# Adapter loops of five engines written out, batch numbers read ahead of SyncE's waits, one role read a pair on TensorE

## The chip, the cores and the metric

The kernel runs on one core of one Trainium2 chip. The metric is the time on the device in microseconds (us). The kernel before took 2073.11 us, the median of three runs (2072.64 to 2078.01).

## The reference, cut to what matters

`reference` chains two layers over `x` of shape (64, 64, 512): 64 batches of 64 tokens of 512 features. The first layer is attention with a projection, a gelu layer of 2048 hidden units (`cW1`, `cW2`), a second gelu layer over the concatenation (`mW1`, `mW2`), and a clip to [0, 1]. The second layer is an adapter whose weights are chosen per batch by a role (one of R = 3 matrices):

```python
h  = einsum('bsh,bhk->bsk', z, W_down[role]) + b_down[role]   # 512 -> 256
u  = einsum('bsk,bkh->bsh', gelu(h), W_up[role]) + b_up[role] # 256 -> 512
y  = z + u
yn = (y - mean(y)) * rsqrt(var(y) + 1e-5)
return yn * gamma[role] + beta[role]
```

Everything is float32. The kernel splits each operand into a high and a low part and forms a product from three matrix products (`mm3`).

## The kernel before, in words

The first layer takes the first 1905 us or so of the program and the diff does not touch it: eight tiles of 512 tokens, worked two at a time in four stages, its instructions written out with no loop. Its result `z` goes to DRAM in batch order (`z_by_batch`), the last two tiles by SyncE's two `store_z` (L444) while the adapter has begun.

The adapter works on pairs of batches with one role: `NPAIR` = 34 pairs of 2 x 64 = 128 token rows. The batches were sorted by role earlier on the chip, so each pair's two batch numbers (`first_t`, `second_t`) and its role (`role_t`) are small integer tables in SBUF. An engine that needs one reads it into a register with `value_load`, which the trace shows as TENSOR_LOAD, FUSED_REGOPS and SEQ_ASSERT on the engine's own sequence. Pair n goes through five engines:

- SyncE (SP), `unit(m)`: waits until slot (m + 2) % 4 of `zs` has been read (`zl_s`, `zf_s`), then `load_z(m + 6)` (L450 reads a batch number and L451 issues the load, twice), then `store_second(m - 1)` (L456 reads a batch number, a wait follows until the first half of that pair has landed, and L459 issues the store of the second half).
- ScalarE (ACT), `unit(n)`: the high part of `ht` (L999), for pair n + 2 the high part `z_hi` (L962) and four instructions `zf` = z + bias (L965) after a role read (L963), and for pair n + 1 the gelu `hs` (L995).
- VectorE (DVE), `unit(n)`: statistics of pair n - 1 (L1599), the low part `ht_lo` (L1630), moments (L1602, L1604), `centre` into `yg` (L1611), `z_lo` of pair n + 2 (L1547), `scale_shift` into `yo` (L1620). `yo` has four slots, and L1620 waits until the second store of pair n - 4 (of its own count) has landed.
- TensorE (PE), `unit(n)`: `turn(n)` reads the role (L1980), waits for `hs`, transposes it (L2001, 2 products) and puts `zf` into the accumulator (L2011, 4 products); `down(n + 1)` reads the role of the next pair, then has one bias product (L1990) and 12 products of `mm3` (L1675 to L1677 into a bank named y); `up(n)` has 6 products of `mm3` (into a bank named x).
- GpSimd (POOL): `inverse_std(n)` (L591) and `store_first(n)` (L595 reads a batch number, L598 issues the store of the first half).

The order on each engine is written by hand, and the engines meet only in counting semaphores. `UNROLL` is 4. Each engine handles its first few pairs in written-out Python, most pairs in one hardware loop (`Fori`) whose body holds four pairs, and the last few written out again: on TensorE the loop takes pairs 4 to 31 in 7 passes, on VectorE 5 to 28, on ScalarE 2 to 29, on GpSimd 0 to 31, on SyncE the units m = 1 to 24 in two loops of 4 and 2 passes. In a loop, table indices and the counts waited for come from registers. All buffers and slots repeat with a period of 1, 2 or 4 pairs.

Of the kernel before, what the change touches and what calls it, by code (L numbers as in the profile page):

```python
# [13 lines left out]
B, S, D = 64, 64, 512  # L14
# [82 lines left out]
NPAIR = B // 2 + 2 * (R // 2)  # L97
NSLOT = 2 * NPAIR
UNROLL = 4
LOOPS = (NPAIR - 3) // UNROLL  # L100


CB1, MB1, BP, CB2, MB2 = 0, JH, 2 * JH, 2 * JH + DC, 2 * JH + 2 * DC
# [3 lines left out]
def program(nc, xT, xk, w1c, w1m, w2c, w2m, wqT, wkT, wvT, wp, bias, target, role,  # L107
# [7 lines left out]
    with ctx:  # L115
# [246 lines left out]
        def _(sp):  # L362
# [80 lines left out]
            def store_z(t, tile, stored):  # L443
                sp.dma_start(z_dram[t * BT:(t + 1) * BT].rearrange("b p f -> p b f"),  # L444
                            tile[:].rearrange("p c n -> p (c n)").rearrange("p (b f) -> p b f", b=BT)
                            ).then_inc(stored, 16)

            def load_z(n, slot):
                for k, table in enumerate((first_t, second_t)):
                    b = sp.value_load(table[0:1, bass.ds(n, 1)], min_val=0, max_val=B - 1)  # L450
                    sp.dma_start(zs[:, slot, k, :, :].rearrange("p c s -> p (c s)"),  # L451
                                 z_dram[bass.ds(b, 1)].rearrange("o p f -> (o p) f")).then_inc(zl[slot], 16)

            def store_second(n, u):

                b = sp.value_load(second_t[0:1, bass.ds(n, 1)], min_val=0, max_val=B - 1)  # L456
                dst = out[bass.ds(b, 1)].rearrange("o s d -> (o s) d")
                sp.wait_ge(a_stored[u % UNROLL], (n - u % UNROLL) * (16 // UNROLL) + 16)
                sp.dma_start(dst, yo[S:2 * S, u % UNROLL, :]).then_inc(b_stored[u % UNROLL], 16)  # L459
# [16 lines left out]
            sp.dma_start(bet[:], beta.to_broadcast([P, R, D])).then_inc(gb_loaded, 16)  # L476

            for n in range(2):
                sp.wait_ge(zl_s, n + 1)
                sp.wait_ge(zf_s, n + 1)  # L480
                load_z(n + 4, n)

            def unit(m, u, load):

                if load:
                    sp.wait_ge(zl_s, m + 3)
                    sp.wait_ge(zf_s, m + 3)
                    load_z(m + 6, (u + 2) % 4)
                if not isinstance(m, int) or m:
                    store_second(m - 1, u + UNROLL - 1)  # L490

            unit(0, 0, True)
# [1 line left out]
            store_z(NT - 2, h2_tile, last_stored[0])  # L494
            sp.wait_ge(z2_ready, DC * NS)
            store_z(NT - 1, h1_tile, last_stored[1])
            sp_loops, sp_early = (NPAIR - 7) // UNROLL, 4
            with sp.Fori(0, sp_early) as k:
                for u in range(UNROLL):
                    unit(k * UNROLL + (u + 1), u + 1, True)  # L500
            sp.wait_ge(last_stored[0], 16)
            sp.wait_ge(last_stored[1], 16)
            with sp.Fori(sp_early, sp_loops) as k:
                for u in range(UNROLL):
                    unit(k * UNROLL + (u + 1), u + 1, True)
            for m in range(sp_loops * UNROLL + 1, NPAIR):
                unit(m, m, m + 6 < NPAIR)
            store_second(NPAIR - 1, NPAIR - 1)
            for u in range(UNROLL):
# [4 lines left out]
        def _(pool):  # L514
# [74 lines left out]
            def inverse_std(n, slot):  # L589
                pool.wait_ge(ve_s, n + 1)  # L590
                nc.gpsimd.tensor_tensor(rstd[:, slot:slot + 1], veps[:, slot:slot + 1], mhalf[:],  # L591
                                        ALU.pow).then_inc(rstd_s, 1)

            def store_first(n, u):
                b = pool.value_load(first_t[0:1, bass.ds(n, 1)], min_val=0, max_val=B - 1)  # L595
                dst = out[bass.ds(b, 1)].rearrange("o s d -> (o s) d")
                pool.wait_ge(yo_s, n + 1)
                pool.dma_start(dst, yo[0:S, u % UNROLL, :]).then_inc(a_stored[u % UNROLL], 16)  # L598

            inverse_std(0, 0)  # L600
            pool_loops = (NPAIR - 2) // UNROLL
            with pool.Fori(0, pool_loops) as k:
                for u in range(UNROLL):
                    store_first(k * UNROLL + u, u)
                    inverse_std(k * UNROLL + (u + 1), (u + 1) % 2)
            for n in range(pool_loops * UNROLL, NPAIR):
                store_first(n, n)
                if n + 1 < NPAIR:
                    inverse_std(n + 1, (n + 1) % 2)
# [40 lines left out]
        def _(act):  # L650
# [302 lines left out]

            def split_z(n, u):

                if isinstance(n, int) and n < 2:
                    act.wait_ge(bu_loaded, 16 * R)
                    act.wait_ge(sorted_s, 3)
                slot = u % 4
                act.wait_ge(zl[slot], (n - slot) * 8 + 32)  # L960
                src = zs[:, slot].rearrange("p k c s -> p c k s")
                nc.scalar.copy(z_hi[:, u % 2].rearrange("p c (k s) -> p c k s", k=2), src).then_inc(zh_s, 1)  # L962
                r = act.value_load(role_t[0:1, bass.ds(n, 1)], min_val=0, max_val=R - 1)  # L963
                for c in range(DC):
                    ins = nc.scalar.activation(zf[:, slot, c, :].rearrange("p (k s) -> p k s", k=2), src[:, c],  # L965
                                               ACT.Identity, bias=bucol[:, bass.ds(r, 1), c])
                ins.then_inc(zf_s, 1)
# [37 lines left out]
            gelu_pair(0, 0)  # L1005
            for n in range(2):
                unit(n, n, True, True)
            with act.Fori(0, LOOPS) as k:
                for u in range(UNROLL):
                    unit(k * UNROLL + (2 + u), 2 + u, True, True)  # L1010
            for n in range(LOOPS * UNROLL + 2, NPAIR):
                unit(n, n, n + 2 < NPAIR, n + 1 < NPAIR)


# [1 line left out]
        def _(dve):  # L1016
# [635 lines left out]
                z2_clip(s, c)  # L1652
            for n in range(3, 5):
                unit(n, n, True, True, False)
            dve_loops = (NPAIR - 7) // UNROLL
            with dve.Fori(0, dve_loops) as k:
                for u in range(UNROLL):
                    unit(k * UNROLL + (5 + u), 5 + u, True, True, True)
            for n in range(dve_loops * UNROLL + 5, NPAIR):
                unit(n, n, n + 2 < NPAIR, True, True)  # L1660
            last = NPAIR - 1
            r = dve.value_load(role_t[0:1, last:last + 1], min_val=0, max_val=R - 1)
# [8 lines left out]
        def _(pe):  # L1671
# [307 lines left out]
            def pair_role(n):  # L1979
                return pe.value_load(role_t[0:1, bass.ds(n, 1)], min_val=0, max_val=R - 1)  # L1980
# [1 line left out]
            def rows(ap, r):  # L1982
                return ap[:, bass.ds(r, 1)].rearrange("p o n -> p (o n)")

            def down(n, u):

                r = pair_role(n)
                pe.wait_ge(zl_s, n + 1)
                ps = d_ps[u % 2][:, 0:KD]
                nc.tensor.matmul(ps, ones2[:], rows(brow[:], r), start=True, stop=False)  # L1990
                for k in range(DC):
                    w = [rows(half[:, :, k, :], r) for half in (wd_hi, wd_lo)]
                    ins = mm3(ps, (z_hi[:, u % 2, k, :], z_lo[:, u % 2, k, :]), w, False, k == DC - 1)
                ins.then_inc(d_mm, 1)

            def turn(n, u):

                r = pair_role(n)
                pe.wait_ge(hgelu_s, n + 1)
                for k in range(KD // P):  # L2000
                    ins = nc.tensor.transpose(ht_ps[u % 2][:, k * P:(k + 1) * P], hs[:, u % 2, k * P:(k + 1) * P],  # L2001
                                              ident[:])
                ins.then_inc(ht_mm, 1)
                ps = u_ps[u % 4]
                if isinstance(n, int) and n < 4:
                    pe.wait_ge(z1_s, (NS - 1) * DC + n + 1)
                else:
                    pe.wait_ge(yg_s, n - 3)
                pe.wait_ge(zf_s, n + 1)
                for k in range(DC):  # L2010
                    nc.tensor.matmul(ps[:, k * P:(k + 1) * P], zf[:, u % 4, k, :], ident[:], start=k == 0,  # L2011
                                     stop=False, is_transpose=True)
                return r

            def up(n, u, r):

                if isinstance(n, int) and n == 0:
                    pe.wait_ge(l1_lo, 2 * R)
                pe.wait_ge(ht_lo_s, n + 1)
                for k in range(KD // P):  # L2020
                    w = [rows(half[:, :, k, :], r) for half in (wu_hi, wu_lo)]
                    cols = slice(k * P, (k + 1) * P)
                    ins = mm3(u_ps[u % 4][:], (ht_hi[:, u % 2, cols], ht_lo[:, u % 2, cols]), w, False,
                              k == KD // P - 1)
                ins.then_inc(u_mm, 1)

            def unit(n, u, d):

                r = turn(n, u)
                if d:  # L2030
                    down(n + 1, u + 1)
                up(n, u, r)

            down(0, 0)
            for n in range(4):
                unit(n, n, True)
            pe_loops = (NPAIR - 5) // UNROLL
            with pe.Fori(0, pe_loops) as k:
                for u in range(UNROLL):
                    unit(k * UNROLL + (4 + u), u, True)  # L2040
            for n in range(pe_loops * UNROLL + 4, NPAIR):
                unit(n, n, n + 1 < NPAIR)


# [46 lines left out]
```

## Time and profile before

| What | Value |
|---|---|
| median of 3 runs | 2073.11 us |
| the profiled execution's own time | 2075.36 us |
| its span | 2073.8 us |
| TensorE busy over the span | 2020.6 us (97%) |
| VectorE, ScalarE, GpSimd busy | 67%, 46%, 5% |
| granted TensorE clock, mean | 0.996 |

The page gives one row for each group of instructions with its busy time, count and mean, and says what ended the idle time ahead of them. The trace can also be asked for a stretch of time, for the chain of waits that ended last in it, and for one engine's instructions in order. The adapter is only the last 160 us or so; the share of busy time over the whole span says almost nothing about it.

### The profile page before, as it was taken

How to read it: one execution, taken by the hardware profiler on the slowest of the kernel's cores; microseconds unless marked ns; L12 is line 12 of the kernel's file. 1: busy time of each engine (PE TensorE's matmuls, PEld its weight loads, DVE VectorE, ACT ScalarE, POOL GpSimd, SP SyncE). 2: the span in 40 equal slices, each digit the busy share in tenths (PEclk: the TensorE clock that was granted, in tenths of full speed). 3: DMA queues.
4: the chain of work that ended last, by engine and by line, in shares of the span. 5: the costliest groups of instructions: out<-in, count | busy, mean ns of one | idle time of the engine just before them, and what ended most of it. 6: DMA issues, size and time to landing. Idle time of an engine off the chain costs nothing.

```text
span 2073.8 us, 28655 instructions
## 1 busy us (share of the span) xinstructions
PE 2020.6 (97%) x9396; PEld 1677.2 (81%) x9397; DVE 1398.5 (67%) x2597; ACT 955.2 (46%) x1977; POOL 99.1 (5%) x184
## 2 busy tenths in 40 slices
PE   7999999999999999999999999999999999999997
PEld 6878888888878888888878888888878888887876
DVE  5676786555777686555777686555677685555886
ACT  4654444433654454333654444333654444334554
POOL 0000000000000000000000000000000000000222
PEclk9999999999999999999999999999999999999999
DMA  4011233215111143215111143215111132114544
GB/s 163 28 52 53 65 129 107 90 49 202 63 51 61 58 136 107 84 54 203 62 51 61 51 142 107 76 62 203 62 52 61 51 122 61 49 44 144 176 123 106
DMA packets 111934, 187.86 MB, mean 91 GB/s; under 512 B 12285, under 2 KB 72192, under 8 KB 107456
## 3 DMA queue, kind: packets, MB, share of 16 engines
q1 hardware_dynamic: 98672, 126.19, 19.4%
q0 software_dynamic: 13136, 60.04, 8.4%
q8 instruction: 72, 1.18, 0.2%
q14 instruction: 54, 0.44, 0.1%
HBM read 145.82 MB, written 40.37 MB: 90 GB/s over the span
## 4 chain that ended last, share of the span: by engine, by line
PE 85%; DVE 7%; SPq 3%; issue 2%; ACT 2%; DMA 1%; ACTq 0%; POOL 0%; DVEq 0%; POOLq 0%
PE y L1675 15%; PE y L1677 15%; PE y L1676 15%; PE x L1675 13%; PE x L1677 12%; PE x L1676 12%; SPq L450 1%; DVE w_lo L1103 1%; PE y L1756 1%; DVE f L1227 1%; PE x L1781 1%; SPq L451 1%; DVE a_forms L1272 1%; DMA w_blocks<-w1c 1%; SPq L459 1%
## 5 line engine op out<-in xcount | busy, mean ns | idle before, releaser
L672 ACT CAST w_hi<-w_blocks 128x512 fp32r<-128x512 f32 (+1 forms) x464 | 231.6, 518 | 131.1 <-PE y L1677 83.6
L1103 DVE TENSOR_TENSOR w_lo<-w_blocks,w_hi 128x512 fp32r<-128x512 f32 (+1 forms) x464 | 249.6, 564 | 56.2 <-ACT w_hi L672 56.2
L1675 PE MATMUL x<-h_hi,w_hi 128*128 128x512 f32 x512 | 199.6, 390 | 3.1 <-ACT f L725 3.1
L1675 PE MATMUL y<-h_hi,w_hi 128*128 128x512 f32 x512 | 199.7, 390 | 1.9 <-ACT p_copy L725 1.9
L1677 PE MATMUL x<-h_hi,w_lo 128*128 128x512 f32 x512 | 199.3, 389 | 0.0
L1677 PE MATMUL y<-h_hi,w_lo 128*128 128x512 f32 x512 | 199.2, 389 | 0.0
L1676 PE MATMUL x<-h_lo,w_hi 128*128 128x512 f32 x512 | 199.2, 389 | 0.0
L1676 PE MATMUL y<-h_lo,w_hi 128*128 128x512 f32 x512 | 199.2, 389 | 0.0
L1675 PE MATMUL y<-a_forms,w_hi 128*128 128x512 f32 x480 | 188.1, 392 | 2.1 <-DVE f L1206 1.2
L1677 PE MATMUL y<-a_forms,w_lo 128*128 128x512 f32 x480 | 186.8, 389 | 0.0
L1676 PE MATMUL y<-a_forms,w_hi 128*128 128x512 f32 x480 | 186.8, 389 | 0.0
L1675 PE MATMUL y<-c_forms,w_hi 128*128 128x512 f32 x448 | 174.3, 389 | 0.0
L1677 PE MATMUL y<-c_forms,w_lo 128*128 128x512 f32 x448 | 174.3, 389 | 0.0
L1676 PE MATMUL y<-c_forms,w_hi 128*128 128x512 f32 x448 | 174.3, 389 | 0.0
L710 ACT CAST w_hi<-w_st 128x512 fp32r<-128x512 f32 x128 | 79.1, 621 | 203.4 <-PE y L1677 109.4
L1675 PE MATMUL x<-a_forms,w_hi 128*128 128x512 f32 x424 | 165.4, 390 | 5.2 <-issue 5.2
L1187 DVE TENSOR_TENSOR h_lo<-f,h_hi 128x512 fp32r<-128x512 f32 x236 | 158.0, 686 | 10.8 <-ACT f L725 10.8
L1677 PE MATMUL x<-a_forms,w_lo 128*128 128x512 f32 x424 | 165.1, 389 | 0.0
L1676 PE MATMUL x<-a_forms,w_hi 128*128 128x512 f32 x424 | 165.0, 389 | 0.0
L1216 DVE TENSOR_TENSOR f<-p_copy,y 128x512 f32<-128x512 f32 x32 | 22.0, 687 | 186.9 <-PE y L1677 186.9
L724 ACT ACTIVATE h_hi<-y,bias_sb 128x512 fp32r<-128x512 f32 x40 | 27.6, 690 | 208.5 <-PE y L1677 208.4
L724 ACT ACTIVATE h_hi<-f,bias_sb 128x512 fp32r<-128x512 f32 x120 | 87.0, 725 | 70.0 <-issue 60.7
(231 smaller groups left out, 4259.9 us busy)
## 6 DMA issues: line engine op xcount, KB each, us to landing
w_blocks<-w1m SPq DMA_DIRECT2D x128, 256.0 KB, 4.2
w_blocks<-w1c SPq DMA_DIRECT2D x64, 256.0 KB, 3.2
w_st<-w2c SPq DMA_DIRECT2D x64, 256.0 KB, 3.3
w_st<-w2m SPq DMA_DIRECT2D x64, 256.0 KB, 4.7
x_hi_lo<-x_halves POOLq DMA_DIRECT2D x6, 2048.0 KB, 11.2
zs<-z_by_batch SPq DMA_DIRECT2D x68, 128.0 KB, 2.1
cms<-f SPq DMA_DIRECT2D x32, 256.0 KB, 2.7
z_cms<-cms POOLq DMA_DIRECT2D x8, 1024.0 KB, 6.4
```

The lines of the kernel that those rows point to most:

```text
L450: b = sp.value_load(table[0:1, bass.ds(n, 1)], min_val=0, max_val=B - 1)
L451: sp.dma_start(zs[:, slot, k, :, :].rearrange("p c s -> p (c s)"), z_dram[bass.ds(b, 1)].rearrange("o p f -> (o p) f")).then_inc(zl[slot], 16)
L459: sp.dma_start(dst, yo[S:2 * S, u % UNROLL, :]).then_inc(b_stored[u % UNROLL], 16)
L672: nc.scalar.copy(w1_hi[:, w % RING, cols], src).then_inc(w1_hi_s, 1)
L710: nc.scalar.copy(w2_hi[:, j, :], w2_st[:, j, :]).then_inc(w2_hi_s, 1)
L724: nc.scalar.activation(hidden_dst(which)[0], src, ACT.Gelu, bias=bias)
L1103: nc.vector.tensor_tensor(w1_lo[:, w % RING, cols], src, f32(w1_hi[:, w % RING, cols]), ALU.subtract).then_inc(w1_lo_s, 1)
L1187: nc.vector.tensor_tensor(lo, half_f32(gi), f32(hi), ALU.subtract).then_inc(hlo_s, 1)
L1216: nc.vector.tensor_tensor(f1[:, 1, :], pc[:, Q % 2, :], GB[Q // NQ % 2][2][:], ALU.add).then_inc(sum_s, 1)
L1675: nc.tensor.matmul(ps, w[0], x[0], start=first, stop=False, skip_group_check=more)
L1676: nc.tensor.matmul(ps, w[0], x[1], start=False, stop=False, skip_group_check=more)
L1677: return nc.tensor.matmul(ps, w[1], x[0], start=False, stop=last, skip_group_check=more)
```

## The change

Every `Fori` of the adapter is gone: the five engines' instruction sequences for all 34 pairs are written out by Python, so the indices and counts are constants. The work of each pair and the slots are the same. Two orders change. On SyncE `load_z` now reads both batch numbers first, then waits for the slot, then issues both loads (the waits have moved from `unit` into `load_z`). On TensorE the role of pair n + 1 is read once, ahead of `turn(n)`, and kept for `up(n + 1)`; before, it was read in `down(n + 1)` and again in `turn(n + 1)`.

```diff
+            def batch_of(table, n):
+                return sp.value_load(table[0:1, n:n + 1], min_val=0, max_val=B - 1)
+
             def load_z(n, slot):
-                for k, table in enumerate((first_t, second_t)):
-                    b = sp.value_load(table[0:1, bass.ds(n, 1)], min_val=0, max_val=B - 1)
+                batches_ = [batch_of(table, n) for table in (first_t, second_t)]
+                if n >= 4:
+                    sp.wait_ge(zl_s, n - 3)
+                    sp.wait_ge(zf_s, n - 3)
+                for k, b in enumerate(batches_):
                     sp.dma_start(zs[:, slot, k, :, :].rearrange("p c s -> p (c s)"),
                                  z_dram[bass.ds(b, 1)].rearrange("o p f -> (o p) f")).then_inc(zl[slot], 16)
 ...
             def unit(m, u, load):
 
                 if load:
-                    sp.wait_ge(zl_s, m + 3)
-                    sp.wait_ge(zf_s, m + 3)
                     load_z(m + 6, (u + 2) % 4)
 ...
-            sp_loops, sp_early = (NPAIR - 7) // UNROLL, 4
-            with sp.Fori(0, sp_early) as k:
-                for u in range(UNROLL):
-                    unit(k * UNROLL + (u + 1), u + 1, True)
-            sp.wait_ge(last_stored[0], 16)
-            sp.wait_ge(last_stored[1], 16)
-            with sp.Fori(sp_early, sp_loops) as k:
-                for u in range(UNROLL):
-                    unit(k * UNROLL + (u + 1), u + 1, True)
-            for m in range(sp_loops * UNROLL + 1, NPAIR):
+            for m in range(1, NPAIR):
+                if m == 4 * UNROLL + 1:
+                    sp.wait_ge(last_stored[0], 16)
+                    sp.wait_ge(last_stored[1], 16)
                 unit(m, m, m + 6 < NPAIR)
 ...
-            with pool.Fori(0, pool_loops) as k:
-                for u in range(UNROLL):
-                    store_first(k * UNROLL + u, u)
-                    inverse_std(k * UNROLL + (u + 1), (u + 1) % 2)
-            for n in range(pool_loops * UNROLL, NPAIR):
+            for n in range(NPAIR):
 ...
-            with act.Fori(0, LOOPS) as k:
-                for u in range(UNROLL):
-                    unit(k * UNROLL + (2 + u), 2 + u, True, True)
-            for n in range(LOOPS * UNROLL + 2, NPAIR):
+            for n in range(2, NPAIR):
 ...
-            with dve.Fori(0, dve_loops) as k:
-                for u in range(UNROLL):
-                    unit(k * UNROLL + (5 + u), 5 + u, True, True, True)
-            for n in range(dve_loops * UNROLL + 5, NPAIR):
+            for n in range(5, NPAIR):
 ...
-            def down(n, u):
-
-                r = pair_role(n)
+            def down(n, u, r):
+
                 pe.wait_ge(zl_s, n + 1)
 ...
             def turn(n, u):
 
-                r = pair_role(n)
                 pe.wait_ge(hgelu_s, n + 1)
 ...
-            down(0, 0)
-            for n in range(4):
-                unit(n, n, True)
-            pe_loops = (NPAIR - 5) // UNROLL
-            with pe.Fori(0, pe_loops) as k:
-                for u in range(UNROLL):
-                    unit(k * UNROLL + (4 + u), u, True)
-            for n in range(pe_loops * UNROLL + 4, NPAIR):
-                unit(n, n, n + 1 < NPAIR)
+            r = pair_role(0)
+            down(0, 0, r)
+            for n in range(NPAIR):
+                if n + 1 < NPAIR:
+                    r_next = pair_role(n + 1)
+                turn(n, n)
+                if n + 1 < NPAIR:
+                    down(n + 1, n + 1, r_next)
+                up(n, n, r)
+                r = r_next
```

## Rows read from the trace of the kernel before

**Rows 1.** VectorE in order of time (start us, us), statistics of pairs 4 and 11

```profile
1945.02 0.70 DVE L1599 BATCH_NORM_STATS2 st<-x 128x6 f32<-128x512 f32 x1 [1.32 <-PE x L1677]
...
1970.71 0.70 DVE L1599 BATCH_NORM_STATS2 st<-x 128x6 f32<-128x512 f32 x1 [0.17 <-PE x L1677]
```

**Rows 2.** The same, statistics of pair 32

```profile
2057.85 0.70 DVE L1599 BATCH_NORM_STATS2 st<-x 128x6 f32<-128x512 f32 x1 [0.64 <-PE x L1677]
```

**Rows 3.** Chain that ended last, 1958 to 2036 us, shares by line

```profile
by line: SPq L450 25.5%; issue 22.5%; SPq L451 17.1%; SPq L459 11.8%; SPq L456 10.0%; DMA zs<-z_by_batch 2.5%; PE x L2011 1.1%; PE y L1675 1.0%; PE y L1990 1.0%; ACTq L963 0.8%; PE y L2001 0.8%; ACT zf L965 0.8%; PE y L1677 0.8%; PE y L1676
```

**Rows 4.** SyncE in order of time, whole span of the loops and after

```profile
1973.50 1.52 SPq L451 DMA_DIRECT2D zs<-z_by_batch  x2
...
1990.47 1.52 SPq L451 DMA_DIRECT2D zs<-z_by_batch  x2
...
2044.38 1.46 SPq L451 DMA_DIRECT2D zs<-z_by_batch  x2
...
2047.95 1.65 SPq L451 DMA_DIRECT2D zs<-z_by_batch  x2
```

**Rows 5.** Line L450, loop units 5 to 24 (duration ns min/median/max)

```profile
L450 SPq TENSOR_LOAD <-first_t x20: 263/494/739, 1955.7 to 2035.6; - x20
```

**Rows 6.** Line L450, written-out units 25 to 27

```profile
L450 SPq TENSOR_LOAD <-first_t x3: 263/269/282, 2039.7 to 2047.2; - x3
L450 SPq TENSOR_LOAD <-second_t x3: 267/272/470, 2040.8 to 2048.3; - x3
```

**Rows 7.** DMA queues, 1980.80 to 1981.30 us, during a slow batch read

```profile
q0 software_dynamic: 29, 0.12, 113.7%
```

**Rows 8.** TensorE in order of time, bias products around a loop's return

```profile
1952.63 0.36 PE L1990 MATMUL y<-brow,ones 128*128 x1
...
1956.63 0.38 PE L1990 MATMUL y<-brow,ones 128*128 x1
```

**Rows 9.** The same, pairs 5 to 7, and the wait ahead of pair 5

```profile
1941.77 0.38 PE L1990 MATMUL y<-brow,ones 128*128 x1 [0.82 <-issue]
...
1945.39 0.36 PE L1990 MATMUL y<-brow,ones 128*128 x1
1949.00 0.38 PE L1990 MATMUL y<-brow,ones 128*128 x1
```

**Rows 10.** Chain in order of time, TensorE, two pairs (start us, us, what)

```profile
2039.34 0.28 issue
2039.63 0.38 PE y L1990
...
2042.60 0.24 PE x L1677
...
2043.49 0.12 PE y L1990
```

**Rows 11.** VectorE in order of time, first and last of pair 6's seven instructions

```profile
1952.26 0.70 DVE L1599 BATCH_NORM_STATS2 st<-x 128x6 f32<-128x512 f32 x1
...
1954.93 0.75 DVE L1620 SCALAR_TENSOR_TENSOR yo<-yg,rstd,bet 128x512 f32<-128x512 f32 x1
```

**Rows 12.** Who waited for whom, 1970 to 2026 us (us in total, times, longest)

```profile
ACT z_hi L962 <- DMA zs<-z_by_batch: 9.8, 13, 1.3
...
DVE yo L1620 <- DMA out<-yo: 4.3, 13, 0.6
```

**Rows 13.** The same, 1944 to 1970 us

```profile
ACT z_hi L962 <- DMA zs<-z_by_batch: 0.4, 1, 0.4
```

**Rows 14.** DMA issues, 1956 to 2044 us, with median us to landing

```profile
zs<-z_by_batch SPq DMA_DIRECT2D x42, 128.0 KB, 2.0
```

**Rows 15.** DMA queues of the whole span, from the page (packets, MB, share)

```profile
q8 instruction: 72, 1.18, 0.2%
```

**Rows 16.** Busy time by stretch: us, PE, PEld, DVE, ACT, POOL (instructions), clock, DMA

```profile
1750.00:1800.00 50.00, 50.00 (x222) 41.41 (x221) 28.96 (x45) 17.33 (x29) 0.00 (x0) 1.00 0.21 64
1970.00:2026.00 56.00, 52.14 (x329) 43.02 (x329) 45.20 (x92) 33.42 (x93) 14.68 (x26) 1.00 0.45 123
```

More of the change, by code:

```diff
@@ L99 @@
 UNROLL = 4
-LOOPS = (NPAIR - 3) // UNROLL
 CB1, MB1, BP, CB2, MB2 = 0, JH, 2 * JH, 2 * JH + DC, 2 * JH + 2 * DC
@@ L454, in store_second @@
             def store_second(n, u):
-                b = sp.value_load(second_t[0:1, bass.ds(n, 1)], min_val=0, max_val=B - 1)
+                b = batch_of(second_t, n)
                 dst = out[bass.ds(b, 1)].rearrange("o s d -> (o s) d")
@@ L478, in _ @@
             for n in range(2):
-                sp.wait_ge(zl_s, n + 1)
-                sp.wait_ge(zf_s, n + 1)
                 load_z(n + 4, n)
@@ L485, in unit @@
                 if load:
-                    sp.wait_ge(zl_s, m + 3)
-                    sp.wait_ge(zf_s, m + 3)
                     load_z(m + 6, (u + 2) % 4)
-                if not isinstance(m, int) or m:
+                if m:
                     store_second(m - 1, u + UNROLL - 1)
@@ L600, in _ @@
             inverse_std(0, 0)
-            pool_loops = (NPAIR - 2) // UNROLL
-            with pool.Fori(0, pool_loops) as k:
-                for u in range(UNROLL):
-                    store_first(k * UNROLL + u, u)
-                    inverse_std(k * UNROLL + (u + 1), (u + 1) % 2)
-            for n in range(pool_loops * UNROLL, NPAIR):
+            for n in range(NPAIR):
                 store_first(n, n)
@@ L954, in split_z @@
             def split_z(n, u):
-                if isinstance(n, int) and n < 2:
+                if n < 2:
                     act.wait_ge(bu_loaded, 16 * R)
@@ L1654, in _ @@
                 unit(n, n, True, True, False)
-            dve_loops = (NPAIR - 7) // UNROLL
-            with dve.Fori(0, dve_loops) as k:
-                for u in range(UNROLL):
-                    unit(k * UNROLL + (5 + u), 5 + u, True, True, True)
-            for n in range(dve_loops * UNROLL + 5, NPAIR):
+            for n in range(5, NPAIR):
                 unit(n, n, n + 2 < NPAIR, True, True)
@@ L2004, in turn @@
                 ps = u_ps[u % 4]
-                if isinstance(n, int) and n < 4:
+                if n < 4:
                     pe.wait_ge(z1_s, (NS - 1) * DC + n + 1)
@@ L2012, in turn @@
                                      stop=False, is_transpose=True)
-                return r
             def up(n, u, r):
-                if isinstance(n, int) and n == 0:
+                if n == 0:
                     pe.wait_ge(l1_lo, 2 * R)
@@ L2025, in up @@
                 ins.then_inc(u_mm, 1)
[L2027 to L2032, printed above, removed]
-            down(0, 0)
-            for n in range(4):
-                unit(n, n, True)
-            pe_loops = (NPAIR - 5) // UNROLL
-            with pe.Fori(0, pe_loops) as k:
-                for u in range(UNROLL):
-                    unit(k * UNROLL + (4 + u), u, True)
-            for n in range(pe_loops * UNROLL + 4, NPAIR):
-                unit(n, n, n + 1 < NPAIR)
+            r = pair_role(0)
[8 more added lines that the diff above has]
+                r = r_next
 def kernel(**inputs):
```

## The prediction

> **What bounds the kernel now.** I first read the page's busy shares and then stretches of it. Ahead of the adapter TensorE is busy 50.00 of 50 us, in the middle of the adapter 52.14 of 56 [rows 16]. So the first 1905 us are bound by TensorE and untouched here, and the question is what bounds a pair of the adapter. The clock row is 1.00 in both stretches, so no part of the sum comes from the clock.
>
> Next, one instruction that occurs once a pair, VectorE's statistics, is a ruler. From pair 4 (1945.02) to pair 32 (2057.85) there are 28 pairs in 112.83 us, 4.03 us each [rows 1, 2]. It is not even: pairs 4 to 11 take 25.69 us for 7, 3.67 each [rows 1], and from there on it is 87.14 us for 21, 4.15 each.
>
> The chain of waits for the slow part names the owner. Of 1958 to 2036 us, 64.4% are SyncE's lines L450, L451, L456 and L459, and most of the 22.5% called "issue" are the steps between its instructions [rows 3]. SyncE waits for nobody there; it is just a long sequence of register work and DMA issues. Its loads come 16.97 us apart per pass of four pairs, 4.24 us a pair [rows 4]. The waits say the same from the other end: between 1970 and 2026 us ScalarE waits 13 times, 9.8 us, for `zs` to land, and `scale_shift` waits 13 times for the second store to land [rows 12]; between 1944 and 1970 us the first of these is one wait of 0.4 us [rows 13]. SyncE started with a lead and used it up.
>
> What is the next bound? TensorE's bias product L1990 comes at 1945.39 and 1949.00, 3.61 us apart [rows 9], with no idle time named. VectorE's pair 6 runs from 1952.26 to 1954.93 + 0.75 = 1955.68, 3.42 us, and then waits for TensorE [rows 11]. So the floors are TensorE 3.61, VectorE about 3.42, SyncE 4.24.
>
> **SyncE written out.** Units 25 to 27 are already written out before, which shows the price directly. The first loads of units 26 and 27 are at 2044.38 and 2047.95, 3.57 us apart with the same three reads and three issues [rows 4]. Against 4.24 that is 0.67 less a pair. Most of that is the loop's register work and its return. But 0.23 of it is not the loop's: the read of the first batch number has a median of 494 ns in the loop and 269 in the written-out units [rows 5, 6]. One slow read, at 1980.80, has 29 packets of the software queue (GpSimd's store) over it, at full share [rows 7]; a written-out unit at the same moment would pay the same, and one read of units 25 to 27 did, 470 ns [rows 6]. So I bound a written-out unit by 3.57 (no slow read) and 3.80 (one in each), 4.03 with two.
>
> Does 3.80 bind? SyncE's lead at the start, by the paces before, was about (4.24 - 3.67) x 7 = 4.0 us, since it lasted from pair 4 to about 11. At 3.80 against TensorE's 3.65 (below) it loses 0.15 x 25 = 3.8 us over the remaining loads, which is just covered. Reading the batch numbers ahead of the wait hides two of them, 0.54 us, but only when SyncE waits, and at this pace it hardly does: I count 0 for it, with 0 and 0.54 a pair as ends. What it is not moved past is a load it could delay: the same three issues follow in the same order, and the wait for the first half's landing (L459) still stands last in the unit, with the next loads behind it; before this wait was long met, because SyncE ran about three pairs late, and it stays so.
>
> A rule of the Trainium skill speaks against this step. "DMA: Bandwidth & Descriptors", section "Latency and other measured facts", gives a register load from memory a floor of about 600 ns. By that a unit with three reads would be an estimated 3.57 + 3 x 0.33 = 4.6 us and SyncE would stay the bound, with no gain. This trace disagrees: 263 to 282 ns for the quickest reads.
>
> **TensorE: one role read, and not in the middle.** Before, `down(n + 1)` reads the role after the four L2011 products. When `hs` came late, the sequence has not run ahead, and the read is exposed: after the last L2011 there are 0.28 us of issue and then an L1990 of 0.38, where the unexposed pair has none and 0.12 [rows 10]. That is 0.54 us, and it makes the bound of such a pair 3.61 + 0.54 = 4.15. In the new order the read stands behind the six products of `up`, of which one takes 0.24 [rows 10], so 1.4 us of array work, where the second read of the pair stood before without a gap. I take the 0.54 as gone; ends 0 (the gap moves to ahead of L2001) and 0.54.
>
> **TensorE, VectorE, ScalarE and GpSimd written out.** A return of TensorE's loop costs up to 4.00 - 3.61 = 0.39 us (L1990 from 1952.63 to 1956.63) [rows 8, 9]. VectorE's and ScalarE's returns lie beside TensorE's 3.61 now, and cost nothing while TensorE is the bound. GpSimd waits most of each pair. So TensorE's pair is 3.61 at best. The early stretch had 3.67 with one return in it, 0.06 a pair; I take 3.65, since a slow read on ScalarE may still make `hs` late by a tenth or two. Ends: 3.61 and 3.80.
>
> **The start.** Statistics of pair 4 waited 1.32 us for TensorE [rows 1], 0.82 of it ahead of L1990 for the role read [rows 9], just as the 1 MB store of `z` ran. I take 0.8 as gained, between 0 and 1.3. Before that VectorE is full with the last clips and covers the rest. **The end**, from pair 32's statistics to the end of the span, 2073.8 - 2057.85 = 15.95 us, was written out and stays.
>
> **Sum.** 28 x (4.03 - 3.65) = 10.6, and 0.8 at the start: 11.4 us off the profiled execution's 2075.36 gives 2064.0. That execution was 2.25 us over the median of 2073.11; taken from the median it is 2061.7. I predict 2062. Its own range: pairs at 3.61 and 1.3 at the start give 28 x 0.42 + 1.3 = 13.1 (2060); pairs at 3.80 and nothing at the start 6.4 (2066.7); one us more each way for the scatter of the runs.
>
> **Rivals.**
>
> 1. SyncE stays the bound. For it: it has the longest sequence, 3.57 to 3.80 against 3.61, and slow reads come at the moments when GpSimd's stores run, which in a steady rhythm can hit the same read each time, as they did in the loop. Two slow reads a unit, 4.03, cost (4.03 - 3.65) x 25 - 4.0 = 5.5 us after the lead. Gain 5.9, time 2067.2. The waits of rows 12 would come back late in the adapter.
> 2. The gap on TensorE stays in half of the pairs, because the read ahead of `turn` is itself waited for. Pairs at 3.61 + 0.27 = 3.88, gain 28 x 0.15 = 4.2 and nothing at the start, 2068.9. Against it: the read that stood there before showed no gap.
> 3. Slower. Written out, the sequences must be fetched. The page counts 72 instruction packets [rows 15], one in 28.8 us; TensorE at 443 products and weight loads in 50 us [rows 16] does about 255 of them in that time. The adapter has 658 in 56 us [rows 16], some 50 a pair, about 70 with its register work (an estimate), so the 24 pairs no longer looped need about 7 more packets on TensorE alone, and about as many together on the others. If TensorE stopped at each for a DMA's time to landing, 2.0 us [rows 14], that is 14 us, and with a few stops of SyncE, say 4 us, the kernel is 6.6 us slower: 2079.7. It decides from 11.4 / 7 = 1.6 us a packet. Against it: the first 1905 us are fetched in the same way with TensorE busy 50.00 of 50 us [rows 16]. The Trainium skill ("Runtime: NRT & Kernel Launch", section "Instruction fetch mechanics") has the next block fetched while the current one runs, mostly hidden; the trace agrees at the lower rate, and does not show this rate for long.
>
> **How the numbers follow.** Forecast 0.70, rival 1 0.17, rival 2 0.08, rival 3 0.05. A change of 0.3%, 6.2 us, is what the runs of this kernel can tell from none. The forecast lies beyond it nearly whole, rival 1 about half, rival 2 rarely: faster 0.79, same 0.16, slower 0.05. Eight in ten: 2059 (3.61 a pair, all of the start, scatter) to 2069 (rivals 1 and 2 reached); the forecast's own is 2059 to 2066.
>
> **What would show it.** Right: statistics of VectorE 3.6 to 3.7 us apart through the whole adapter; no wait of ScalarE for `zs` of more than a few tenths; the chain of the adapter made of TensorE's lines; L1990 with no gap; SyncE's loads paced by TensorE or still ahead. Wrong: a pace of 3.8 or more with SyncE's lines in the chain (rival 1), gaps ahead of L2001 or L1990 (rival 2), or single stops of over 1 us with an instruction packet beside each (rival 3). A change in the first 1905 us would show that I missed something altogether.

## The result and the profile after

The changed kernel takes 2065.33 us, the median of five runs (2064.27 to 2068.34), against 2073.11 (2072.18 to 2078.01) for the kernel before beside it: a ratio of 0.9962 with a 95% interval of 0.9950 to 0.9974. Two further sets of five runs gave 0.9963 (0.9950 to 0.9977) and 0.9959 (0.9946 to 0.9972). So it is faster by 0.38%, some 8 us, more than the 0.3% that can be told from none. 2062 was forecast. One run each of two kernels below had a lower clock (0.87 and 0.62 of full speed; 2203 and 3038 us) and is left out of their medians.

The profiled execution took 2064.27 us, 11.1 less than the one of before. The page of the changed kernel (busy us, share, instructions; then the queues that fetch instructions: packets, MB, share):

```profile
span 2062.7 us, 28119 instructions
PE 2013.5 (98%) x9396; PEld 1676.9 (81%) x9396; DVE 1396.2 (68%) x2596; ACT 952.0 (46%) x1976; POOL 99.0 (5%) x183
q8 instruction: 78, 1.28, 0.3%
q14 instruction: 62, 0.51, 0.1%
```

TensorE has the same 9396 products; q8 had 72 packets before [rows 15]. The ruler of the prediction, VectorE's statistics once a pair, now in line L1586. Pairs 4, 22 to 25 and 31:

```profile
1945.06 0.70 DVE L1586 BATCH_NORM_STATS2 st<-x 128x6 f32<-128x512 f32 x1
...
2009.95 0.70 DVE L1586 BATCH_NORM_STATS2 st<-x 128x6 f32<-128x512 f32 x1 [0.18 <-PE x L1660]
2013.53 0.70 DVE L1586 BATCH_NORM_STATS2 st<-x 128x6 f32<-128x512 f32 x1
2017.84 0.70 DVE L1586 BATCH_NORM_STATS2 st<-x 128x6 f32<-128x512 f32 x1 [0.23 <-PE x L1660]
2021.44 0.70 DVE L1586 BATCH_NORM_STATS2 st<-x 128x6 f32<-128x512 f32 x1 [0.20 <-PE x L1660]
...
2043.48 0.70 DVE L1586 BATCH_NORM_STATS2 st<-x 128x6 f32<-128x512 f32 x1 [0.20 <-PE x L1660]
```

Pair 32 follows at 2047.09. The 28 pairs take 102.03 us, 3.64 each, where they took 112.83 [rows 1, 2]. Most are 3.59 apart, and VectorE waits a fifth of a us for TensorE in nearly every one; pair 24 is 4.31 after pair 23 (2013.53 to 2017.84) and pair 28 is 4.01 after 27. The adapter from its first `z_hi` (1909.37, before 1908.11) to pair 4 takes 35.7 us, before 36.9. The first layer, untouched, ends 1.26 us later in this execution.

Who waited for whom from 1970 to 2026 us, the stretch of [rows 12]:

```profile
DVE st L1586 <- PE x L1660: 2.8, 15, 0.2
ACT z_hi L952 <- DMA zs<-z_by_batch: 1.7, 4, 1.0
PEld y L1982 <- ACT hs L985: 0.9, 1, 0.9
```

ScalarE waits 4 times for `zs` and not 13, 1.7 us and not 9.8; VectorE no longer waits for its stores, and no gap ahead of the bias product is left. SyncE in order of time, two units, which answer to [rows 4], and its reads of the first batch number (1956 to 2036 us, ns min/median/max), which answer to [rows 5]:

```profile
1957.84 0.50 SPq L464 DMA_DIRECT2D out<-yo  x1
1959.69 0.87 SPq L456 DMA_DIRECT2D zs<-z_by_batch  x2
1961.31 0.50 SPq L464 DMA_DIRECT2D out<-yo  x1
1963.17 0.87 SPq L456 DMA_DIRECT2D zs<-z_by_batch  x2
```

```profile
L448 SPq TENSOR_LOAD <-first_t x22: 262/273/420, 1958.4 to 2035.9; - x22
```

These two units are 3.48 us apart, a little under TensorE's 3.59. But SyncE is not gone: in this execution two marks of rival 1 are there, a wait of 1.0 us for `zs`, and the chain that ended last. In 1999 to 2022 us, around the late pair 24, it is still SyncE's own:

```profile
by line: SPq L448 38.8%; SPq L456 23.1%; issue 22.3%; SPq L464 16.7%; SPq L454 0.4%; SPq L501 0.1%
```

### The profile page after: what moved, and what is told of

Its sections match the earlier page's. It is cut to its first block, busy times and chain, and to the rows that moved or that the text cites. A ratio compares the mean times of both kernels' runs of the same rounds, so it can differ in the third digit from the quotient of the medians.

```text
span 2062.7 us, 28119 instructions
## 1 busy us (share of the span) xinstructions
PE 2013.5 (98%) x9396; PEld 1676.9 (81%) x9396; DVE 1396.2 (68%) x2596; ACT 952.0 (46%) x1976; POOL 99.0 (5%) x183
## 4 chain that ended last, share of the span: by engine, by line
PE 81%; DVE 9%; SPq 4%; issue 2%; DMA 2%; ACT 2%; DVEq 0%; POOL 0%; ACTq 0%; POOLq 0%
PE y L1658 14%; PE y L1660 14%; PE y L1659 14%; PE x L1658 12%; PE x L1660 12%; PE x L1659 12%; SPq L448 2%; DVE w_lo L1090 1%; PE y L1739 1%; SPq L456 1%; DVE f L1214 1%; PE x L1764 1%; DVE c_forms L1252 1%; DVE a_forms L1259 1%; DMA w_blocks<-w1c 1%
## 5 line engine op out<-in xcount | busy, mean ns | idle before, releaser
L1174 DVE TENSOR_TENSOR h_lo<-f,h_hi 128x512 fp32r<-128x512 f32 x236 | 157.9, 686 | 11.1 <-ACT f L715 11.1
```

The source lines that it names most:

```text
L1174: nc.vector.tensor_tensor(lo, half_f32(gi), f32(hi), ALU.subtract).then_inc(hlo_s, 1)
```

## The experiments

In the table, "ratio" is to the kernel before on the same chip, "pairs 4 to 32" and "unit" (mean distance of SyncE's second stores of pairs 3 to 26, with whatever SyncE waited in it) are from each profile.

| Kernel | median us | ratio (95%) | pairs 4 to 32 | unit |
|---|---|---|---|---|
| before | 2073.1 to 2075.8 | 1 | 112.8 | 4.19 |
| changed | 2065.3 | 0.9962 (0.9950 to 0.9974) | 102.0 | 3.71 |
| changed, second time | 2066.6 | 0.9963 (0.9950 to 0.9977) | 105.7 | 3.90 |
| changed, third time | 2066.5 | 0.9959 (0.9946 to 0.9972) | 101.1 | 3.66 |
| only SyncE written out | 2065.8 | 0.9961 (0.9948 to 0.9975) | 102.4 | 3.69 |
| only TensorE written out | 2072.7 | 0.9995 (0.9986 to 1.0004) | 110.1 | 4.02 |
| two role reads | 2063.6 | 0.9945 (0.9932 to 0.9959) | 102.4 | 3.68 |
| two role reads again | 2065.0 | 0.9957 (0.9944 to 0.9969) | 101.3 | 3.63 |
| waits first | 2064.2 | 0.9961 (0.9948 to 0.9974) | 101.1 | 3.68 |
| extra read | 2080.6 | 1.0034 (1.0021 to 1.0047) | 117.3 | 4.26 |
| SyncE and TensorE | 2066.0 | 0.9966 (0.9953 to 0.9979) | 103.7 | 3.78 |
| second number kept | 2062.9 | 0.9948 (0.9936 to 0.9961) | 101.2 | 3.47 |
| kept, again | 2062.1 | 0.9937 (0.9924 to 0.9949) | 100.8 | 3.47 |
| kept, only SyncE written out | 2065.7 | 0.9956 (0.9943 to 0.9969) | 102.4 | 3.54 |

**The changed kernel again.** No edit.

> The changed kernel a second time, unchanged. From pair 4 to pair 32 its first profile had 102.0 us against 112.8 before, the start of the adapter was 1.2 us shorter and the first layer, which no line of the diff touches, 1.26 us longer; that profile was 11.1 us under the one of before, while the medians differ by 7.8. Theory A (the adapter gains about 12 us in every execution, and the medians differ by less because executions scatter by 3 to 6 us in the first layer): the adapter takes 102 +- 1 us for these pairs again and the first layer is off by another amount, of either sign. Rival B (the longer program costs 1 us or more in the first layer each time): the first layer is 1.2 us longer than before again. Time: A 2062 to 2067, B 2064 to 2067.

The first layer ended at 1907.75, earlier than before's 1908.11 and not 1.2 us later: rival B, a fixed cost in every execution, falls. Over the 13 profiles after the one of before it ends between 1907.5 and 1913.0 (the changed kernel alone: 1909.4, 1907.8, 1911.0). A smaller cost on average is not excluded: 10 of the 13 end it later than before's only profile did. But Theory A's 102 +- 1 us fell too: 105.7. All from pair 19 on. VectorE's statistics of pairs 24 to 29 in that execution:

```profile
2017.22 0.70 DVE L1586 BATCH_NORM_STATS2 st<-x 128x6 f32<-128x512 f32 x1
2020.98 0.70 DVE L1586 BATCH_NORM_STATS2 st<-x 128x6 f32<-128x512 f32 x1
2024.82 0.70 DVE L1586 BATCH_NORM_STATS2 st<-x 128x6 f32<-128x512 f32 x1 [0.20 <-PE x L1660]
2028.90 0.69 DVE L1586 BATCH_NORM_STATS2 st<-x 128x6 f32<-128x512 f32 x1
2033.09 0.70 DVE L1586 BATCH_NORM_STATS2 st<-x 128x6 f32<-128x512 f32 x1
2037.28 0.69 DVE L1586 BATCH_NORM_STATS2 st<-x 128x6 f32<-128x512 f32 x1
```

That is 3.8 to 4.2 us a pair. SyncE at that time, and the queues from 2023 to 2025.5 us:

```profile
2019.49 0.87 SPq L456 DMA_DIRECT2D zs<-z_by_batch  x2
2021.11 0.50 SPq L464 DMA_DIRECT2D out<-yo  x1
2022.98 2.13 SPq L456 DMA_DIRECT2D zs<-z_by_batch  x2
2025.87 0.49 SPq L464 DMA_DIRECT2D out<-yo  x1
```

```profile
q8 instruction: 1, 0.02, 3.1%
q14 instruction: 2, 0.02, 1.5%
zs<-z_by_batch SPq DMA_DIRECT2D x2, 128.0 KB, 3.1
```

A pair of issues takes 2.13 us where the one ahead took 0.87, beside a packet of q8, and the loads need 3.1 us to land. In this execution five issues were of 1.16 to 1.60 us, each within 0.5 us of a q8 packet. Over SyncE's 23 units its issues took 5.8 us more than at their usual 0.34 and 0.49 (2.3 in the first profile), its reads 2.4 us more than at 0.27 (1.5 in the first). So I formed theory D: the packets eat SyncE's lead.

**Only SyncE written out.** SyncE's block of the changed kernel, the other four of before:

```diff
 SyncE: batch_of, load_z, unit and the loop as in the changed kernel
 GpSimd, ScalarE, VectorE, TensorE: Fori and two role reads as before
```

> Only SyncE is written out, with both batch numbers read ahead of the waits; TensorE, VectorE, ScalarE and GpSimd keep their loops and TensorE its two role reads. Theory A (SyncE's sequence of 4.24 us a pair was the bound and TensorE comes next at 3.61): a pair takes about 3.61 plus a quarter of a loop's return of 0.39, 3.71 us, so pairs 4 to 32 take 104 us, 2 more than in the changed kernel, and the time is 2 to 3 us over it. Rival C (TensorE's exposed role read and its loop did most of it): a pair stays at 3.9 or more, 109 us and over, with gaps ahead of L1990 in most pairs; the time is 7 or more over the changed kernel.

102.4 us and level with the changed kernel: theory A, and even quicker than its 104. Nothing in its adapter waited for SyncE, and its chain from 1958 to 2026 us is all TensorE. Statistics around a return of the loops:

```profile
1979.03 0.70 DVE L1595 BATCH_NORM_STATS2 st<-x 128x6 f32<-128x512 f32 x1
1982.63 0.70 DVE L1595 BATCH_NORM_STATS2 st<-x 128x6 f32<-128x512 f32 x1
1986.22 0.70 DVE L1595 BATCH_NORM_STATS2 st<-x 128x6 f32<-128x512 f32 x1 [0.19 <-PE x L1673]
1990.06 0.70 DVE L1595 BATCH_NORM_STATS2 st<-x 128x6 f32<-128x512 f32 x1 [0.42 <-PE x L1673]
```

3.60, 3.59, then 3.84: this return costs 0.25 us, not 0.39.

**Only TensorE written out.**

```diff
 TensorE: down(n, u, r), turn, up and the loop as in the changed kernel
 SyncE, GpSimd, ScalarE, VectorE: Fori as before
```

> Only TensorE is written out, with its one role read ahead of the turn; SyncE and the others keep their loops. Theory A: SyncE stays the bound at 4.24 us a pair once its lead is gone; pairs 4 to 32 take 110 to 112 us (the first seven and the last seven gain a little), the time is within 3 us of before. Rival C: a pair comes down to 3.7 or less, about 104 us, and most of the gain is there.

110.1 us and no gain beyond the interval; rival C falls. ScalarE waits as in [rows 12] (1970 to 2026 us):

```profile
ACT z_hi L962 <- DMA zs<-z_by_batch: 9.9, 13, 1.0
...
DVE yo L1620 <- DMA out<-yo: 5.8, 8, 2.0
```

**Two role reads, written out** (run twice).

```diff
-            def down(n, u, r):
+            def down(n, u):
+                r = pair_role(n)
-            def turn(n, u):
+            def turn(n, u):
+                r = pair_role(n)
```

> The changed kernel, all written out, but TensorE reads the role twice a pair as before, once ahead of the turn and once between the turn and the down products. The prediction took 0.54 us for each pair in which that second read is exposed. Theory A (it is exposed only where the gelu is late, and with SyncE out of the way it is not late): pairs of 3.60 to 3.62 and no gap ahead of the bias product, 102 to 103 us for pairs 4 to 32, same time as the changed kernel within 1 us. Rival C (it is exposed as often as before): gaps of 0.28 us and a pace of 3.8 to 4.15, 107 to 116 us.

> All written out, with TensorE's two role reads a pair as before, once more, since its first median was 2 to 3 us under the changed kernel's while its profile was not. Theory A: no difference but the 0.8 us of the start: level with the changed kernel of this call or 1 us over it, pairs 4 to 32 like its. Rival K (the second read on TensorE helps, for instance by spacing its instruction blocks otherwise): 2 us or more under it again.

Theory A both times, 102.4 and 101.3 us: nearly every pair takes 3.60 or 3.61. The chain of the second run in one steady pair (start us, us):

```profile
1993.27 0.22 PE y L1984 x2
1993.49 0.44 PE x L1994 x4
1993.93 0.12 PE y L1973
```

No gap ahead of the bias product, though the role is read there: the 0.54 us of [rows 10] is gone without the edit meant to remove it. Only the start is longer, 36.6 and 36.3 us and not 35.4 to 35.8. Its first median was the lowest of the kernels beside it, its second 1.5 us under the changed kernel's; both are within the intervals, so rival K is not shown.

In the first of the two runs pairs 16 and 20 are late, 4.54 and 4.05 us after the ones ahead. No issue was stretched for them. Two loads issued in 0.33 us each, at 1983.39 and 1998.21, had a q8 packet over them (from 1984.82 and 1998.82) and took 3.67 and 4.00 us to land. The first is in the chain of pair 16:

```profile
1983.39 3.67 DMA zs<-z_by_batch
```

So a late landing by itself can hold a pair up, when SyncE's lead is short.

**Waits first.**

```diff
-                batches_ = [batch_of(table, n) for table in (first_t, second_t)]
                 if n >= 4:
                     sp.wait_ge(zl_s, n - 3)
                     sp.wait_ge(zf_s, n - 3)
-                for k, b in enumerate(batches_):
+                for k, table in enumerate((first_t, second_t)):
+                    b = batch_of(table, n)
```

> The changed kernel, all written out, but SyncE waits for the slot first and then reads and issues one load after the other, as before the change. The prediction gave the new order nothing. Theory A: SyncE hardly waits for a slot, so the same within 1 us, pairs of 3.6; its unit stays 3.5 us. Rival G (the order matters, since the first load leaves 0.55 us earlier now or the reads hide behind waits): 0.2 us a pair or more in one direction, 5 us.

Level. The new order is worth nothing here.

**One more read.**

```diff
+                batch_of(first_t, n)
                 b = batch_of(second_t, n)
                 dst = out[bass.ds(b, 1)].rearrange("o s d -> (o s) d")
```

> The changed kernel with one more batch number read in each SyncE unit, its value unused. Theory A and D: a unit is 3.48 + 0.55 = 4.03 us, more than TensorE's 3.59; after a lead of about 4 us is used up the pairs come 4.0 us apart or more, pairs 4 to 32 take 108 to 110 us and the time is 6 to 8 us over the changed kernel: most of what the change gained. Rival F (SyncE's length is not what counts once the loops are gone): within 1 us of the changed kernel.

Rival F falls, and so does the size of mine: some 15 us over the changed kernel (by the two ratios), slower than before. Its waits (1970 to 2026 us), and two of its quick units:

```profile
ACT z_hi L953 <- DMA zs<-z_by_batch: 13.9, 13, 1.6
PEld y L1983 <- ACT hs L986: 10.1, 12, 1.6
DVE yo L1608 <- DMA out<-yo: 9.9, 11, 2.2
```

```profile
2022.02 0.48 SPq L465 DMA_DIRECT2D out<-yo  x1
2023.86 0.86 SPq L456 DMA_DIRECT2D zs<-z_by_batch  x2
2026.02 0.48 SPq L465 DMA_DIRECT2D out<-yo  x1
```

The quick unit is 4.00, as expected (2022.02 to 2026.02), but the mean from 1958.09 to 2056.01 (23 units) is 4.26: slow reads add a quarter of a us (17 of the 92 took over 0.4 us; no issue took over 0.51). And the first late pair is already pair 8 (4.72 us after pair 7). So SyncE's lead is not 4 us but 1 to 2: four pairs at 4.26 against 3.6 lose 2.6, and 1.1 of it shows at pair 8 (an estimate).

**SyncE and TensorE written out, the other three in loops.**

```diff
 SyncE, TensorE: as in the changed kernel
 GpSimd, ScalarE, VectorE: Fori as before
```

> SyncE and TensorE written out, the other three in loops. It differs from the run with only SyncE written out in TensorE alone. Theory D: TensorE's 16 KB instruction packets come back, about seven after pair 8, and with them SyncE issues of 0.6 us and more beside several of them and zs landings of 2.5 us and more; the start is 1.2 us shorter, each return of TensorE's loop (0.2 us a pass) is gone, and some late pairs are 0.3 to 1 us late; the sum is a draw, within 2 us of that run. Rival H (the slow issues belong to SyncE's own instruction blocks or to those of the other three engines): none of them here, pairs 4 to 32 in 101 us, 2 to 3 us faster.

The load issues of SyncE, 1956 to 2042 us (ns min/median/max), first with only SyncE written out, then with TensorE too:

```profile
L457 SPq DMA_DIRECT2D zs<-z_by_batch x46: 328/338/352, 1956.3 to 2037.7; - x46
```

```profile
L457 SPq DMA_DIRECT2D zs<-z_by_batch x46: 328/344/1698, 1955.8 to 2038.9; - x46
```

Theory D. With TensorE in its loop not one of 46 issues is over 352 ns and q8 has no packet from 1956 to 2036 us; with TensorE written out q8 has five there, and five issues of 0.78 to 1.70 us between 1956 and 2042 us each start within 1 us of such a packet. So q8 fetches for TensorE, and the long issues come with these packets. What the written-out TensorE wins in loop returns and at the start, it loses here: the times are level.

But a packet is not enough. With only TensorE written out q8 has five packets too, each with a load issue of SyncE started inside it, and none of those issues is long (1956 to 2036 us, and 1956 to 2042):

```profile
q8 instruction: 5, 0.08, 0.4%
L451 SPq DMA_DIRECT2D zs<-z_by_batch x44: 337/344/357, 1956.3 to 2041.6; - x44
```

What differs is the distance to the issue ahead. In the new order the second load starts 0.53 us after the first; in the old one a read lies between, and it is 1.1 us or more. In the nine profiles with the new order and TensorE written out, 19 second loads were started inside a q8 packet, and all 19 took 0.58 to 1.60 us; of 17 first loads started inside one, none took over 0.46. In the two with the old order (only TensorE written out, and waits first) it is 2 of 11 loads. So part of the price seems to come from the change's own order. Why is not shown, and "waits first", which spaces the loads again, gained no time by it.

**The second batch number kept** (run twice).

```diff
                 batches_ = [batch_of(table, n) for table in (first_t, second_t)]
+                seconds[n] = batches_[1]
...
-                b = batch_of(second_t, n)
+                b = seconds.pop(n)
```

> The changed kernel, but SyncE keeps the register with the second batch number from the load of pair n until the store of pair n, so a unit has two reads instead of three. Theory D (in the changed kernel SyncE's written-out unit of 3.48 us is so near TensorE's 3.59 that each block of instructions fetched for TensorE, which stretches a SyncE issue to 0.6 to 1.6 us and a zs landing from 2.1 to 2.5 or more, eats its lead, and late pairs wait): a unit of about 2.9 us wins the lead back between the blocks; the stretched issues are still there, but no pair after the tenth is over 3.7 us apart, pairs 4 to 32 take 101 to 102 us, and the time is 1 to 4 us under the changed kernel. Rival E (the late pairs wait for the landing itself, not for SyncE's turn): the stalls of 0.4 to 0.7 us stay at the blocks, no difference.

> The kernel that keeps the second batch number in a register, once more. Theory D: 101 to 102 us for pairs 4 to 32 again and no stall, 1 to 4 us under the changed kernel of this call. Rival E (no difference beyond scatter): within 1 us of it or over it.

Both times 101.2 us or less and no pair after the sixth over 3.62. In the second run six packets of q8 fall between 1956 and 2036 us and SyncE's issues still reach 988 ns beside them, but nobody waits for it (1970 to 2026 us, all waits of over 0.2 us in total but GpSimd's):

```profile
ACT ht_hi L992 <- PE y L1985: 18.3, 15, 1.2
...
DVE st L1589 <- PE x L1663: 2.9, 16, 0.2
```

Its chain from 1958 to 2026 us:

```profile
by line: PE y L1661 13.4%; PE y L1663 13.3%; PE y L1662 13.2%; PE x L1661 13.1%; PE x L1662 13.0%; PE x L1663 12.8%; PE x L1995 11.9%; PE y L1985 6.1%; PE y L1975 3.4%
```

TensorE throughout. 2062.07 (2061.00 to 2062.42) stood beside the changed kernel's 2066.49 (2064.73 to 2067.93): 4.4 us less, and no run of the one reaches any of the other. It beats both kernels. How much of the 4.4 us is SyncE's slack is not shown: the two profiles beside each other differ by 3.7 us, and 3.5 of it lies in the first layer (1907.5 against 1911.0), 0.3 in pairs 4 to 32. What the profiles show is that the late pairs are gone, against the changed kernel's first two runs.

**The changed kernel a third time, and the kept number with only SyncE written out.**

> The changed kernel once more, to stand beside the kernels of this call. Theory D: SyncE and TensorE run nearly level, so from one execution to the next pairs 4 to 32 take 102 to 106 us (102.0 and 105.7 so far), depending on which SyncE issues meet TensorE's instruction packets. Rival I (the 105.7 was an outlier): 101 to 102.5 us. The medians' gain over before 7 to 9 us either way.

> The second batch number kept, and only SyncE written out; the other four engines in their loops, so hardly any instruction packets in the adapter. Theory D: with SyncE at 2.9 us a unit nothing waits for it, and what is left against the kept version written out everywhere are TensorE's loop returns of 0.22 us a pass, 6 of them, and the start with the exposed role read, 1.2 us: about 102.5 us for pairs 4 to 32 and 2 to 3 us over it. Rival J (the packets cost even the kept version something, by slower landings): level with it.

101.1 us: neither theory alone, since the three profiles now say 102.0, 105.7 and 101.1. Long issues are in all three (five, seven and six over 580 ns from 1936 to 2050 us). They differ in length: over SyncE's 23 units they cost 2.3, 5.8 and 2.1 us. The other kernel's adapter came as theory D had it, 102.4 us and a start of 37.0. Its time is 3.7 us over the kept version written out and not 2 to 3; the profiles differ by 6.4, of which 3.0 is the first layer (1910.5 against 1907.5), so the excess is scatter as far as these runs tell.

## Why the prediction was right

**The bound, and the sum for the profiles.** SyncE's length was the bound: written out alone it gives the whole gain, TensorE alone none, and a read more than takes it back. The pace forecast was 3.65, measured 3.64, 3.78 and 3.61; the start forecast 0.8, measured 1.2; the sum 11.4 from profile to profile, measured 11.1. That the sum fits so closely is partly luck: the two terms gave 10.8 and 1.2, which is 12.0, the end gave 0.3 (15.61 us, before 15.95), and the first layer took 1.3 back. In the other two profiles the two terms give 8.2 and 13.2.

**The base of the sum: mis-sized.** Medians differ by 7.8, 7.8 and 9.3 us. I took the 11.4 off the median, though the profiled execution was 2.25 us above it. If that surplus lay in the adapter, the median execution had less to gain. That it did is argued, not shown: the first layer of that profile ended at 1908.11, earlier than in 10 of the 13 profiles since, and executions of before went down to 2071.31, which from no first layer under 1907.5 leaves 3 us or more less for adapter and end. No second profile of before was taken, so it stays open how its adapter varies. Two to four of the 11.4 us are in this step or in the scatter; a first layer that ends later on average, as above, is a third way to lose some.

**SyncE's lead: wrong.** I put it at 4.0 us from the paces; the extra read shows 1 to 2. One part of the difference is that writing out TensorE brings pair 4 forward by 1.2 us, which the paces of before could not show; the rest is open. With a mean unit of 3.66 to 3.90 it is used up in some executions (rival 1 in part, with its mark, waits of ScalarE for `zs` late in the adapter). The unit's bounds of 3.57 to 3.80 held as a mean in two of the three executions (3.71, 3.90, 3.66); single units go down to 3.48.

**Reading ahead of the wait: right at 0.**

**TensorE's role read: right in size, wrong in cause.** I gave the edit 0.54 us in each pair with the gap. The gap closes when `hs` is no longer late, with two reads as with one. The edit is worth 0.6 to 1.2 us at the start, once. Rival 2 did not occur.

**Loop returns.** In the two kernels that keep TensorE's loop and do not wait for SyncE the later returns cost 0.2 to 0.3 us, the first ones up to 0.5; I had 0.39 as the upper end.

**Rival 3, the fetched instructions.** In size it did not come: 6 packets more of q8, and TensorE's pace is 3.59 to 3.60 across six of them in the second run with the number kept. But the fetch has a price I did not look for: it falls on SyncE's issues and on the landings, and through so short a lead on late pairs. The Trainium skill ("Runtime: NRT & Kernel Launch", section "Instruction fetch mechanics") calls the cost of a block boundary mostly hidden. For TensorE itself the traces agree, by the pace just given. Of its neighbours the section says nothing, and there the price is: up to 1.7 us for an issue of 0.34.

## What to carry to other kernels

An engine that only issues transfers can be the bound of a loop: count its register reads, its index arithmetic and its issues as time, and compare the sum with the busiest engine's pace. When two engines come out within a few per cent, take more off the slower queue (here one read a unit) rather than trust the tie, since disturbances fall on the one without slack. Take a gain from one profile off that profile's own time, and ask where its distance to the median lies before it is taken off the median.

## What the runs showed of the hardware

- A DMA issue on SyncE of 0.33 to 0.35 us can take 0.6 to 1.7 us beside a 16 KB instruction packet of TensorE (328/338/352 without such packets, up to 1698 with). It hit the load that followed another by 0.53 us (19 of 19 started inside a packet), and no first load (0 of 17).
- Loads of 128 KB that had a q8 packet in flight landed after a median of 2.5 us (changed kernel) and 2.9 (its second run), the others after 2.2 and 2.1. The longest landing beside one took 4.4 us (second run with two role reads).
- A register read from SBUF takes 0.27 us on SyncE, and often about 0.5 where packets of GpSimd's queue lie over it, as in [rows 5, 7]: in the kernel before, from pair 3 to 26, all 19 reads of over 0.4 us had more than ten such packets over them, and so had three of the 49 quick ones.
